# Dense layer of one block: the projection and norm ahead of it and both norms behind it in the same block, token tile by token tile

## The reference

```python
def _self_output(h, residual, w, b, g, be):
    h = h @ w + b
    h = h + residual
    mu = jnp.mean(h, axis=-1, keepdims=True)
    var = jnp.mean(jnp.square(h - mu), axis=-1, keepdims=True)
    return (h - mu) * jax.lax.rsqrt(var + LN_EPS) * g + be
...
x = _self_output(sa, x, so_w, so_b, so_g, so_be)
inter = jax.nn.gelu(x @ fi_w + fi_b, approximate=False)       # fi_w is 256 x 1024
x = _self_output(inter, x, fo_w, fo_b, fo_g, fo_be)           # fo_w is 1024 x 256
```

## Time and profile before

| what | us |
|---|---|
| median of 3 runs | 1773.76 (1770.83 to 1776.09) |
| the profiled execution | 1771.14 |
| its span in the profile | 1769.3 |
| PE, DVE, ACT, POOL busy | 1653.6, 1136.0, 863.2, 244.8 |

### The profile page before, as it was taken

The page is one execution under the profiler, slowest core; times in us unless marked ns, Lnnn a source line. Parts: engine busy times, 40 slices in busy tenths (PEclk is TensorE's granted clock), DMA queues, the critical chain, the costliest instruction groups (busy, mean ns, idle before and its releaser), DMA issues. The chain is left out here.

```text
span 1769.3 us, 36593 instructions
## 1 busy us (share of the span) xinstructions
PE 1653.6 (93%) x12571; PEld 1002.6 (57%) x12579; DVE 1136.0 (64%) x1997; ACT 863.2 (49%) x1777; POOL 244.8 (14%) x323
## 2 busy tenths in 40 slices
PE   7999999999999998868999999799999999989698
PEld 3444445445454545544868999444445444546597
DVE  5777788888888856536452111388888888836311
ACT  2222227777777775512531111257777777746232
POOL 1422220000000000000202444220000000000000
PEclk9999999999999999989898999989999999999699
DMA  5578656434343408000046999654443434130052
GB/s 193 184 194 216 203 161 118 72 54 71 54 71 59 66 4 182 1 0 1 0 156 221 328 312 296 206 91 67 60 68 56 70 54 71 19 97 2 26 180 93
DMA packets 145830, 193.60 MB, mean 109 GB/s; under 512 B 27593, under 2 KB 119260, under 8 KB 139712
## 3 DMA queue, kind: packets, MB, share of 16 engines
q1 hardware_dynamic: 139064, 188.30, 43.6%
q0 software_dynamic: 4608, 2.18, 0.8%
q10 hardware_dynamic: 2064, 1.87, 0.3%
HBM read 155.42 MB, written 39.97 MB: 110 GB/s over the span
## 5 line engine op out<-in xcount | busy, mean ns | idle before, releaser
L1280 ACT ACTIVATE probs<-ps 128x512 f32<-128x512 f32 x1024 | 558.5, 599 | 181.4 <-PE ps L1186 169.0
L1306 DVE TENSOR_REDUCE top<-ps 128x1 f32<-128x1024 f32 x504 | 594.1, 1220 | 61.6 <-PE ps L1165 48.8
L1186 PE MATMUL ps<-qst,kst 105*128 105x256 bf16 x2048 | 353.9, 276 | 6.9 <-DVE qst L1311 1.5
L1165 PE MATMUL ps<-kst,qst 105*128 105x512 bf16 x1008 | 307.7, 388 | 5.3 <-DVE top L1306 3.5
L1186 PEld LDWEIGHTS ps<-qst,kst 105*128 105x128 bf16 x2048 | 170.2, 100 | 227.5 <-ACT probs L1280 86.4
L1200 PE MATMUL ps_o<-probs,vst 128*32 128x256 f32 x4096 | 274.1, 385 | 2.3 <-ACT probs L1280 2.3
L1200 PEld LDWEIGHTS ps_o<-probs,vst 128*32 128x32 f32 x4096 | 106.8, 109 | 113.3 <-issue 51.2
L2219 PE MATMUL ps_h<-xe,vall 128*128 128x80 f32 x1024 | 155.2, 273 | 0.0
L2219 PEld LDWEIGHTS ps_h<-xe,vall 128*128 128x128 f32 x1024 | 142.0, 199 | 0.0
L395 POOL COPY vst<-vall 128x512 f32 (+1 forms) x64 | 39.4, 616 | 698.0 <-PE ps_o L1200 695.2
L1165 PEld LDWEIGHTS ps<-kst,qst 105*128 105x128 bf16 x1008 | 88.6, 99 | 64.4 <-issue 29.0
(11 more groups left out here) (397 smaller groups left out, 2026.7 us busy)
## 6 DMA issues: line engine op xcount, KB each, us to landing
kst<-kd SPq DMA_DIRECT2D x372, 128.0 KB
kd<-probs SPq DMA_DIRECT2D x64, 384.0 KB, 2.8
vall<-in_L_ffn_wg_dram SPq DMA_DIRECT2D x32, 512.0 KB
vall<-in_L_ffn_wu_dram SPq DMA_DIRECT2D x32, 512.0 KB
vall<-in_L_ffn_wd_dram SPq DMA_DIRECT2D x32, 512.0 KB
w<-in_L_ffn_w_dram SPq DMA_DIRECT2D x16, 1024.0 KB, 5.6
vd<-square_weights SPq DMA_DIRECT2D x16, 512.0 KB, 4.1
vall<-vd SPq DMA_DIRECT2D x16, 512.0 KB, 6.0
```

What stands on the lines that cost most here:

```text
L1165: mm = pe.matmul(ps1[:, slot1(m, u), x * 512:(x + 1) * 512], qst[:, m, qt * P:(qt + 1) * P], kst[:, m, c * W1 + x * 512:c * W1 + (x + 1) * ...
L1186: mm = pe.matmul(ps2[:, SCORES2[u], x, :], kst[:, m, kt * P:(kt + 1) * P], qst[:, m, :], start=True, stop=True)
L1280: nc.scalar.activation(probs[:, u % SLOTS, :, :], ps2[:, SCORES2[u], :, :], ACT.Exp).then_inc(probs_ready, 1)
L1306: v.tensor_reduce(top[:, b, qt, c:c + 1], ps1[:, slot1(m, u), :], AX, ALU.max).then_inc(mx, 1)
```

## The change

The five blocks become one, a new `dense_ffn`, which has the steps of `project_and_normalize` at its start.

- Tokens go through the dense layer in two halves of 256 (tiles 0 and 1, tiles 2 and 3). `hidden(0, f)` starts when tiles 0 and 1 are normed, turned and copied; tiles 2 and 3 are turned between its matmuls. Then come two slices of the second half, the second product of tiles 0 and 1, the other six slices, and the second product of tiles 2 and 3. `ps_h` has three places in use instead of four; the matmuls of the first product are 256 columns wide instead of 512.
- The wait for the weights is a wait on PE's queue.
- The norms behind the dense layer run per tile: `out_moments`, `centre`, `add_to_x`, `centre`, `normalize_both`. The gain multiplies the centred tensor before the root is known; the shift and x are added beforehand on POOL (`shifted`), as are the residual and the bias (`added`).
- The second layer norm and the RMS norm share one root: `rsqrt(var * (1 + RMS_EPS) + RMS_EPS * LN_EPS)`, so the moments are taken once. The epsilons are ACT's bias (`eps`, set by POOL at the start; ACT waits for it before its first copy) and are no longer added on DVE.
- Three matmuls of no use stand ahead of each turn, in place of the 16.

```diff
+    with ExitStack() as st:
+        ps_h = (ps_t[:, 0, 0:NH], ps_t[:, 1, 0:NH], ps_o[:, 2, 0:NH])
+        ps_out = [ps_o[:, t, 0:D] for t in (0, 1, 3, 2)]
...
+            @block.gpsimd
+                g.memset(eps[:, 0:1], LN_EPS).then_inc(eps_set, 1)
+                g.memset(eps[:, 1:2], RMS_EPS * LN_EPS).then_inc(eps_set, 1)
+                for t in range(NT):
+                    g.tensor_tensor(added[:, 0, t, :], xn[:, t, :], bias[:, :], ALU.add).then_inc(bias_added, 1)
+                for t in range(NT):
+                    g.tensor_tensor(shifted[:, t, :], x[:, t, :], out_shift[:, :], ALU.add).then_inc(next_added, 1)
+                for t in range(NT):
+                    pool.wait_ge(done, t + 1)
+                    g.tensor_tensor(added[:, 1, t, :], xn[:, t, :], fo_b[:, :], ALU.add).then_inc(next_added, 1)
...
+            @block.tensor          (turn, project, stay_busy as in project_and_normalize)
+                def hidden(half, f):
+                    n = half * NF + f
+                    if n >= 3:
+                        pe.wait_ge(active, n - 2)
+                    for c in range(C):
+                        mm = pe.matmul(ps_h[n % 3], fi[:, c, f * P:(f + 1) * P],
+                                       dstT[:, c, half * NH:(half + 1) * NH], start=(c == 0), stop=(c == C - 1))
+                    mm.then_inc(h_made, 1)
+                def out(t):
+                    for f in range(NF):
+                        if t % 2 == 0:
+                            pe.wait_ge(active, t // 2 * NF + f + 1)
+                        mm = pe.matmul(ps_out[t], hT[:, f, t * P:(t + 1) * P], fo[:, f, :],
+                                       start=(f == 0), stop=(f == NF - 1))
+                    mm.then_inc(out_made, 1)
...
+                for t in range(2):
+                    stay_busy(ps_x[:, 1, :, :].rearrange("p c n -> p (c n)"), 3)
+                    turn_normed(t, done, x_turned)
+                stay_busy(ps_x[:, 1, :, :].rearrange("p c n -> p (c n)"), 3)
+                pe.wait_ge(loading[0], loading[1])
+                pe.wait_ge(x_copied, 1)
+                for f in range(NF):
+                    hidden(0, f)
+                    if f in (1, 3):
+                        turn_normed(2 + f // 2, done, x_turned)
+                pe.wait_ge(x_copied, 2)
+                for f in range(AHEAD):          (AHEAD is 2)
+                    hidden(1, f)
+                out(0)
+                out(1)
+                for f in range(AHEAD, NF):
+                    hidden(1, f)
+                out(2)
+                out(3)
+                for t in range(NT):
+                    stay_busy(ps_t[:, 0, :], 3)
+                    turn_normed(t, n_done, n_turned)
...
+            @block.scalar          (first_root, the four copies of srcT, then)
+                for t in range(NT - 1):
+                    root(0, t)
+                copy_x(0, x_turned)
+                root(0, NT - 1)
+                for f in range(3):
+                    gelu(0, f)
+                copy_x(1, x_turned)
+                for f in range(3, NF):
+                    gelu(0, f)
                 for f in range(NF):
+                    gelu(1, f)
+                for t in range(NT):
+                    for i in range(1, 3):
+                        root(i, t)
+                    if t % 2:
+                        copy_x(t // 2, n_turned)
...
+            @block.vector
+                def add_to_x(t):
+                    scale(1, t)
+                    link(v.scalar_tensor_tensor(out=other[:, t, :], in0=centred[:, t, :], scalar=rstd[:, 1, t:t + 1],
+                                                in1=shifted[:, t, :], op0=ALU.mult, op1=ALU.add))
+                    moments(2, t, other)
+                def normalize_both(t):
+                    scale(2, t)
+                    v.tensor_scalar(xn[:, t, :], scaled[:, t, :], rstd[:, 2, t:t + 1], None, ALU.mult).then_inc(n_done, 1)
+                project_moments(0)
+                for t in range(1, NT):
+                    project_moments(t)
+                    normalize(t - 1)
+                normalize(NT - 1)
+                for t in range(2):
+                    out_moments(t)
+                    centre(1, t, total, centred, out_gain)
+                for t in range(2):
+                    add_to_x(t)
+                    centre(2, t, other, scaled, rms)
+                for t in range(2):
+                    normalize_both(t)
+                for t in range(2, NT):
+                    out_moments(t)
+                    centre(1, t, total, centred, out_gain)
+                    add_to_x(t)
+                    centre(2, t, other, scaled, rms)
+                    normalize_both(t)
```

More of the change, by code:

```diff
@@ L769 @@
 BUSY_MATMULS = 16
[L772 to L853, removed]
@@ L1645, in _, with turn @@
             @block.tensor
             def _(pe):
-                for f in range(NF):
-                    if f >= 4:
-                        pe.wait_ge(active, f - 3)
+                def turn(t):
+                    if t >= 2:
+                        pe.wait_ge(copied, t - 1)
                     for c in range(C):
-                        mm = pe.matmul(ps_h[:, f % 4, :], fi[:, c, f * P:(f + 1) * P], xT[:, c, :],
+                        mm = pe.transpose(ps_t[:, t % 2, c * P:(c + 1) * P], src_tile(t, c), pr.cf("ident"))
+                    mm.then_inc(turned, 1)
@@ L1652, in _, with project @@
+                def project(t):
+                    pe.wait_ge(copied, t + 1)
+                    for c in range(C):
+                        mm = pe.matmul(ps_o[:, t, 0:D], srcT[:, t, c * P:(c + 1) * P], weight[:, c, :],
                                        start=(c == 0), stop=(c == C - 1))
                     mm.then_inc(made, 1)
-                pe.wait_ge(active, NF)
-                for t in range(NT):
-                    for f in range(NF):
-                        mm = pe.matmul(ps_o[:, t, :], hT[:, f, t * P:(t + 1) * P], fo[:, f, :],
-                                       start=(f == 0), stop=(f == NF - 1))
@@ L1659, in _, with stay_busy, turn_normed @@
-                mm.then_inc(out_made, 1)
+                def stay_busy(bank, n):
+                    for _ in range(n):
+                        pe.matmul(bank, pr.cb("identb"), pr.constsb[:, 0:512], start=True, stop=True)
+                def turn_normed(t, sem, signal):
+                    pe.wait_ge(sem, t + 1)
+                    for c in range(C):
+                        mm = pe.transpose(ps_x[:, t // 2, c, (t % 2) * P:(t % 2 + 1) * P], xn[:, t, c * P:(c + 1) * P],
+                                          pr.cf("ident"))
+                    mm.then_inc(signal, 1)
@@ new lines, in copy_x, with gelu @@
+                def copy_x(pair, sem):
+                    act.wait_ge(sem, 2 * pair + 2)
+                    nc.scalar.copy(dstT[:, :, pair * 2 * P:(pair + 1) * 2 * P], ps_x[:, pair, :, :]).then_inc(x_copied, 1)
+                def gelu(half, f):
+                    n = half * NF + f
+                    act.wait_ge(h_made, n + 1)
+                    nc.scalar.activation(hT[:, f, half * NH:(half + 1) * NH], ps_h[n % 3], ACT.Gelu,
+                                         bias=fi_b[:, f:f + 1]).then_inc(active, 1)
@@ new lines, in out_moments, with scale, centre @@
+                def out_moments(t):
+                    dve.wait_ge(out_made, t + 1)
+                    dve.wait_ge(next_added, NT + t + 1)
+                    link(v.tensor_tensor(total[:, t, :], ps_out[t], added[:, 1, t, :], ALU.add))
+                    moments(1, t, total)
+                def scale(i, t):
+                    dve.wait_ge(std_ready[i], t + 1)
+                    link(v.reciprocal(rstd[:, i, t:t + 1], std[:, i, t:t + 1]))
+                def centre(i, t, src, dst, by):
+                    dve.wait_ge(var_ready[i], t + 1)
+                    link(v.scalar_tensor_tensor(out=dst[:, t, :], in0=src[:, t, :], scalar=mv[:, i, t, 0:1],
+                                                in1=by[:, :], op0=ALU.subtract, op1=ALU.mult))
@@ new lines, in normalize @@
+                def normalize(t):
+                    centre(0, t, total, centred, gain)
+                    scale(0, t)
+                    v.scalar_tensor_tensor(out=xn[:, t, :], in0=centred[:, t, :], scalar=rstd[:, 0, t:t + 1],
+                                           in1=shift[:, :], op0=ALU.mult, op1=ALU.add).then_inc(done, 1)
+                def add_to_x(t):
[3 more added lines that the diff above has]
+                    moments(2, t, other)
```

79 lines of the change are left out of this document (55 added, 24 removed).

## The result

| | before | after |
|---|---|---|
| median | 1773.76 us | 1754.93 us (1753.48 to 1756.83, 4 runs) |
| the profiled execution | 1771.14 | 1755.31 |
| its span | 1769.3 | 1753.5 |

The ratio is 0.9895, with a 95% interval of 0.9878 to 0.9913. The forecast was 1755.5, with 1752 to 1759 for the forecast itself and 1750 to 1762 over all cases, so both the time and its sign hold. The changed kernel measured again beside two others gave 1754.56, 0.9905 [0.9889, 0.9922].

The account below looks back on a forecast made before the run. PE's path was taken as the bound, with DVE's solo to go beside it. Savings of 3.4 before, 3.2 in and 10.3 us behind the dense layer made 16.9: 1754.2 or 1756.9 by base, forecast 1755.5, range 1752 to 1759.

Parts of the forecast that it names:

- Part 1: PE's first turn to the dense layer's first matmul: 11.14 us instead of 14.53, since only tiles 0 and 1 are needed.
- The epsilons: First norm on DVE: no longer adding them saves some 0.2 us per tile, taken as -0.3 us.
- ACT's wait for the memsets: Before ACT's first copy: waiting for POOL's two memsets costs 0.1 to 0.5 us, taken as +0.4.
- POOL's sums: First norm: 12 sums instead of 4 slow four DVE instructions with two SBUF inputs by 0.25 us each, +1.0.
- Part 2: Both dense-layer products on PE: 128 records at 0.2175 us plus two turns, 28.3 us at the full clock.
- Part 3: Norms, from the second product's end to the clamped attention's first matmul: 10.9 us, against 21.70 before.
- The stall of tile 2's root: Behind the dense layer: the root stands on ACT behind the copy of turned tiles 0 and 1, a stall of 1.05 us.
- The low clock's +0.5: Clamped attention's first records: more of them at clock 0.50 would cost 0 to 1.2 us, taken as +0.5.
- Full blocking by POOL: Rival for the first norm: four DVE instructions each wait a whole POOL sum, 2.8 us instead of 1.0; 1757.3 us, chance 8%.
- The table load: Before the first root behind the last Gelu: 1.30 us without a drain, against the skill's 1283 ns plus 1380 ns drain.
- The clock's rival: Rival for the dense layer: thin PE work before it lowers the clock, costing 2.8 us; 1758.3 us, chance 15%.
- the slower side: Rival for the dense layer: the full clock never returns, products take 56.6 us; 1783.8 us, chance 2%.

Follow-up runs that it names:

- e1_wait_all: Changed kernel with the norms behind the dense layer waiting for all four tiles of the second product: 1762.3 us, last part 19.34 us.
- e3_quiet: Changed kernel with POOL's eight later sums after the first norm and ACT's wait for the epsilons after its second copy: 9.58 us to the dense layer instead of 10.36.
- e10_no_fill_early: Changed kernel without the twelve matmuls of no use ahead of the dense layer: products 29.99 us instead of 28.31, the stretch before them 11.51 instead of 10.36.
- e6_late_copy: Changed kernel with ACT copying the turned tiles 0 and 1 after tile 2's two roots: 1752.2 us, last part 9.97 us instead of 10.83.
- e5_long_pool: Changed kernel with POOL's four sums of x and the shift as one long instruction: 10.96 us to the dense layer; the centring that met it took 1.60 us.

## Why the prediction was right

- **What bounds.** It took PE's stream, with nothing to save in the matmuls themselves, and DVE's solo of 18 us as what could go under it. e1_wait_all shows the second by undoing it: 8.5 us.
- **Part 1** was forecast 0.8 too long (11.14 against 10.36). All three corrections had the right sign and the wrong size. The epsilons brought about 0.5, not 0.3, because three of them stood ahead of tile 1's last step and the forecast counted two: DVE takes tile 2's moments before it centres tile 1 (740.12 in the timeline before). From bn_aggr's start to the next instruction it is 0.30, 0.29 and 0.29 us before, and 0.16, 0.10 and 0.10 after. ACT's wait for the memsets cost 0.23 (first copy 1.60 us after PE's first turn, 1.37 before), not 0.4: a memset of one column takes 0.10 us, where I had the nearest row's 0.21. POOL's sums cost DVE 0.18, 0.15 and 0.15 on three of four instructions, 0.48 where the term was 1.0 (against e3_quiet's own rows 0.21, 0.15 and 0.17). e3_quiet undid these two terms together: 0.78. The other way, the forecast had left out most of the 0.15 us between the end of the copy and the first matmul.
- **Part 2** is exact: 28.31 against 28.3, 128 records of 256 columns and two turns, no gap, full clock. The assumption on the clock held, and e10_no_fill_early shows what it hung on: without the fillers the products lose 1.7 us, less than the 2.8 that the rival had for them.
- **Part 3**: 10.83 against 10.9. The stall of tile 2's root was forecast at 1.05 and is 0.89 in the row; without it (e6_late_copy) the part is 0.86 shorter. The low clock's +0.5 behind it was +0.54 in the 8 records, and +0.35 in the second profile.
- **The rivals.** Full blocking by POOL is what e5_long_pool shows, but the rival's price was wrong: three of the four DVE instructions met a POOL sum of 0.7 us, each with less than 0.4 us of it left, and lost 0.15 to 0.18 each, not a whole 0.7. The table load had no drain. The clock's rival did not come true, nor did the slower side: the products at half clock would have taken 56.6 us by the forecast's sum, and they took 28.3.
- **The total** is right partly by luck. The stretch saved 18.3 where 17.4 stood in the sum ahead of the clock's 0.5, and the median moved by 18.8; the forecast of 1755.5 was placed between two bases 2.6 us apart. The stretch alone was under-forecast by 0.8 us, nearly all of it in part 1, and the choice of base was worth more than that.

## What to carry to other kernels

When PE and DVE each have a long solo, cut the work into tiles and put the first solo's end under the second; then the tail is what the slower engine has left when the other ends, here about 4.0 us of DVE per tile. Look for an order in which the slower engine starts as early as it can and never stops (all of the first product, then one tile after the other), rather than one that only halves the layer. Behind that come the small ones, all visible as one row each: a root queued behind a copy (0.9), a clock that falls while PE waits (about 2), and an engine pair that excludes each other (0.5).

## What the runs showed of the hardware that I had not expected

- A DVE instruction with two SBUF inputs that starts beside a POOL instruction reading SBUF ends 0.28 us after it (1.60 us for one of 0.45, beside POOL's 2.35). In this stretch of all profiles there are 30 meetings in which POOL's sum had 0.3 us or more left, and the distance was 0.28 to 0.29 us in each. The bn_stats, with one SBUF input, and the sum of PSUM and SBUF kept their time. Through short POOL instructions the loss was 0.15 to 0.18 each.
- One f32 sum of 1024 columns on POOL took 2.35 us, where four of 256 took 2.79 undisturbed.
- With the fillers gone, the clock was at 0.50 at the dense layer's start, behind a row in which PE was busy for 0.44 of 2 us; it was also at 0.50 within the projection, as it was in one profile with the fillers.
- An ACT root whose bias is a column took 0.29 us, where the one without took 0.20. Most are hidden under DVE's centring; the first behind the table load is not.
